# Loading vectors as rows, halving a wait, and reordering the opening of a one-core transformer-block kernel

## What is computed

```python
mod = (silu(c) @ wmod).reshape(4, 6, 1, 512)
sa, ca, ga, sb, cb, gb = (mod[:, i] for i in range(6))
ga, gb = sign-keeping max(|.|, 0.25) of each
h = layernorm(x) * (1 + ca) + sa
x = x + ga * attn_ref(h)      # ln1, shift-mix, r/k/v, out; then ln2, shift-mix, r2/k2/v2
h = layernorm(x) * (1 + cb) + sb
x = x + gb * ffn_ref(h)       # shared expert + top 2 of 8 experts
```

## Time and profile before

| | us |
|---|---|
| median of 3 runs (lowest, highest) | 1719.45 (1712.07, 1720.55) |
| the profiled execution's own time | 1702.0 |
| its span | 1700.3 |
| busy in it: TensorE, VectorE, ScalarE, GpSimd | 1643.6, 1326.2, 770.3, 417.9 |
| mean granted clock of TensorE | 0.993 |

### The profile page before, as it was taken

One profiled execution on the slowest core, in us unless ns is written; L12 is line 12 of the kernel. 1 busy time (PEld: TensorE's weight loads), 2 busy tenths in 40 slices (PEclk: granted clock), 3 DMA queues, 4 the chain that ended last, 5 costly groups with the idle time before them and its releaser, 6 DMA issues.

```text
span 1700.3 us, 26873 instructions
## 1 busy us (share of the span) xinstructions
PE 1643.6 (97%) x8817; PEld 1426.7 (84%) x8817; DVE 1326.2 (78%) x2553; ACT 770.3 (45%) x1138; POOL 417.9 (25%) x505
## 2 busy tenths in 40 slices
PE   4899999999989999999999999999999999999998
PEld 1578788888768888888888888999999999998997
DVE  3999999998698788888788775777777777776872
ACT  2444434333445555454545423555555555552331
POOL 2254444343322111323232351000000000006740
PEclk9999999999999999999999999999999999999999
DMA  9622222322544443655554689788878888866861
GB/s 317 222 76 93 80 99 74 99 74 75 202 149 154 151 149 123 223 183 201 180 197 173 223 318 312 240 287 298 286 259 279 284 299 285 266 219 215 277 209 38
DMA packets 138980, 335.32 MB, mean 197 GB/s; under 512 B 20568, under 2 KB 20568, under 8 KB 133232
## 3 DMA queue, kind: packets, MB, share of 16 engines
q1 hardware_dynamic: 103904, 248.09, 43.6%
q10 hardware_dynamic: 24720, 52.21, 8.6%
q0 software_dynamic: 10240, 33.56, 5.7%
HBM read 230.21 MB, written 103.60 MB: 196 GB/s over the span
## 4 chain that ended last, share of the span: by engine, by line
PE 73%; DVE 15%; DMA 4%; issue 3%; SPq 2%; ACT 2%; POOL 1%; DVEq 0%; ACTq 0%; POOLq 0%
PE bank L701 17%; PE bank L703 17%; PE bank L702 17%; PE bank L712 5%; PE bank L2412 5%; PE bank L2410 5%; PE bank L2411 5%; PE bank L2405 2%; DVE stage L1714 2%; DVE mix L1793 1%; DVE xm_lo L1799 1%; DMA expert_in_rows<-y_rows 1%; SPq L798 1%; DMA mod_rows<-ca_rows 1%; PE bank L2394 1%
## 5 line engine op out<-in xcount | busy, mean ns | idle before, releaser
L701 PE MATMUL bank<-gu_hi,ex_x_hl 128*128 128x352 f32 x1080 | 359.9, 333 | 0.1
L703 PE MATMUL bank<-gu_hi,ex_x_hl 128*128 128x352 f32 x1080 | 348.5, 323 | 0.0
L702 PE MATMUL bank<-gu_lo,ex_x_hl 128*128 128x352 f32 x1080 | 348.4, 323 | 0.0
L1281 POOL DMA_INDIRECT raw<-expert_out_rows,out_slots x64 | 74.9, 1170 | 536.7 <-DMA expert_out_rows<-y_rows 513.0
L701 PEld LDWEIGHTS bank<-gu_hi,ex_x_hl 128*128 128x128 f32 x1080 | 203.7, 189 | 0.4 <-issue 0.3
L702 PEld LDWEIGHTS bank<-gu_lo,ex_x_hl 128*128 128x128 f32 x1080 | 204.0, 189 | 0.0
L703 PEld LDWEIGHTS bank<-gu_hi,ex_x_hl 128*128 128x128 f32 x1080 | 203.3, 188 | 0.0
L1888 DVE TENSOR_TENSOR hid<-bank,sg_t 128x352 f32<-128x352 f32 x135 | 70.2, 520 | 126.8 <-PE bank L703 107.7
L2410 PE MATMUL bank<-dn_hi,hid_hi 128*128 128x512 f32 x405 | 161.7, 399 | 3.9 <-DVE hid_lo L1892 3.9
L2412 PE MATMUL bank<-dn_hi,hid_lo 128*128 128x512 f32 x405 | 160.0, 395 | 0.0
L2411 PE MATMUL bank<-dn_lo,hid_hi 128*128 128x512 f32 x405 | 158.7, 392 | 0.0
(11 more groups left out here) (257 smaller groups left out, 3835.9 us busy)
## 6 DMA issues: line engine op xcount, KB each, us to landing
raw<-in_ex_gu SPq DMA_DIRECT2D x40, 1408.0 KB, 6.5
raw<-in_ex_dn SPq DMA_DIRECT2D x40, 512.0 KB, 4.7
ex_x<-expert_in_rows SPq DMA_DIRECT2D x71, 256.0 KB, 6.3
expert_out_rows<-y_rows ACTq DMA_DIRECT2D x71, 256.0 KB, 6.1
h_rows<-h_t SPq DMA_DIRECT2D x64, 256.0 KB, 2.6
h_turned<-h_hl ACTq DMA_DIRECT2D x32, 512.0 KB, 3.0
ex_x_hl<-h_turned ACTq DMA_DIRECT2D x32, 512.0 KB, 3.7
x_t<-in_x SPq DMA_DIRECT2D x32, 256.0 KB, 2.7
```

The source lines that it names most:

```text
L701: pe.matmul(acc, act_hi[i], w_hi[i], start=(i == 0), stop=False)
L702: pe.matmul(acc, act_hi[i], w_lo[i], start=False, stop=False)
L703: last = pe.matmul(acc, act_lo[i], w_hi[i], start=False, stop=(i == chunks - 1))
L1281: pool.indirect_dma_start(rows[:, pair % 2, a, :], None, ys_d, bass.IndirectOffsetOnAxis(ap=out_slots[:, k, n:n + 1], axis=0)).then_inc(ar ...
```

## The change

1. The nine small vectors are loaded as 36 rows of 128 contiguous elements (4 rows each), all before anything else on ScalarE; TensorE turns the 36 rows with one transpose, and ScalarE copies the result to `vecs`.
2. The first third of `wmod` has two semaphores; the products of `sa` and `ca` start on the first two chunks when these are there.
3. SyncE's queue: tile 1 of x right after the first third of `wmod`; tiles 2 and 3 of x when tiles 0 and 1 were scaled, ahead of the other two thirds of `wmod`, with `v` between them and `o`, `u` among them; the rows of batches 1 to 3 in step 0; stores of the next two modulation rows in step 1 and the weights of channel mixing in step 2.
4. VectorE: for t < 0, `mixes` of tile t + 1 goes ahead of `scaled` of tile t + 3, and `x_stats` comes last; `r` and `k` are split in step -2, `v` in -1.
5. ScalarE and TensorE: `r`, `k` split after the modulation rows; the products of `ga`, `sb` in step -2, of `cb` in step 0 and of `gb` in step 1.

```diff
+        vec_rows = ga_rows[0:9 * C, 0:P]
...
+        wmod_first_in = sem("wmod_first_in")
...
-        MOD_BANK = {SA: psum[0], CA: psum[1], GA: psum[3], SB: psum[4], CB: psum[5], GB: psum[7]}
-        MOD_TURN = {SA: 1, CA: 2, GA: 5, SB: 6, CB: 7, GB: 8}
-        SPREAD_TURN = {SA: 3, CA: 4}
-        MOD_COPIED = {SA: 1, CA: 2, SB: 5, CB: 6}
+        MOD_BANK = {SA: psum[0], CA: psum[1], GA: psum[3], SB: psum[4], CB: psum[7], GB: psum[7]}
+        VECS_TURNED, VECS_COPIED = 1, 1
+        MOD_TURN = {SA: 2, CA: 3, GA: 6, SB: 7, CB: 8, GB: 9}
+        SPREAD_TURN = {SA: 4, CA: 5}
+        MOD_COPIED = {SA: 2, CA: 3, SB: 6, CB: 7}
...
-        SPLIT_IN_STEP = {-4: ["r", "k"], -2: ["v"], 0: ["o"], 5: ["r2"], 8: ["k2"], 11: ["v2"]}
+        SPLIT_IN_STEP = {-2: ["r", "k"], -1: ["v"], 0: ["o"], 5: ["r2"], 8: ["k2"], 11: ["v2"]}
...
                 for c in range(C):
...
-                                 io["wmod"][c * P:(c + 1) * P, 2 * q * D:2 * (q + 1) * D]).then_inc(wmod_in[q], 16)
+                                 io["wmod"][c * P:(c + 1) * P, 2 * q * D:2 * (q + 1) * D]
+                                 ).then_inc(wmod_first_in if q == 0 and c < C // 2 else wmod_in[q], 16)
             def load_weight(w):
...
+            sp.dma_start(x_t[:, 1, :], x_d[P:2 * P, :]).then_inc(x_in[1], 16)
...
-            sp.dma_start(x_t[:, 1, :], x_d[P:2 * P, :]).then_inc(x_in[1], 16)
-            load_wmod(1)
-            load_weight("v")
-            load_wmod(2)
-            load_weight("o")
-            sp.dma_start(u_bc[:], io["u"].partition_broadcast(P)).then_inc(u_in, 16)
             for m in (SA, CA):
...
-            sp.wait_ge(mod_out, 32)
-            for b in range(1, B):
-                sp.dma_start(flat(mod1[:, b]), mod_d[b, 0:2 * D].partition_broadcast(P)).then_inc(mod1_in, 16)
+            load_weight("v")
+            sp.wait_ge(*lnh_vec.done(1, "scaled"))
+            sp.dma_start(x_t[:, 1, :], x_d[3 * P:4 * P, :]).then_inc(x_in[1], 16)
+            load_wmod(1)
+            sp.dma_start(u_bc[:], io["u"].partition_broadcast(P)).then_inc(u_in, 16)
+            load_weight("o")
+            load_wmod(2)
             def later_mod(t):
                 if t.only(0):
+                    sp.wait_ge(mod_out, 32)
+                    for b in range(1, B):
+                        sp.dma_start(flat(mod1[:, b]), mod_d[b, 0:2 * D].partition_broadcast(P)).then_inc(mod1_in, 16)
+                if t.only(1):
...
+                if t.only(2):
...
                     for w in W2:
...
-                if t.only(2):
...
             def load_x(t):
-                if t.pair is None and t.n < 3:
+                if t.pair is None and t.n < 4:
...
                 if t.back(2).real():
...
             def load_vector(i):
-                act.dma_start(vecs[:, i, :], io[names[i]].rearrange("(c p) -> p c", p=P),
-                              allow_slow_non_contiguous=True).then_inc(vec_in, 16)
+                act.dma_start(vec_rows[i * C:(i + 1) * C, :], io[names[i]].rearrange("(c p) -> c p", p=P)).then_inc(vec_in, 16)
             def split_hi(w):
...
-            for i in (G1, B1, MUR, MUK, MUV):
+            for i in range(len(names)):
...
-            split_hi("r")
-            mod_row(SA)
-            split_hi("k")
-            mod_row(CA)
+            act.wait_ge(mod_mm, VECS_TURNED)
+            act.activation(vecs[:].rearrange("p i c -> p (i c)"), psum[7][:, 0:9 * C], ACT.Copy).then_inc(mod_act, 1)
+            for m in (SA, CA):
+                mod_row(m)
             for m in (SA, CA):
...
-            act.wait_ge(vec_in, 80)
-            for i in (G2, B2, MUR2, MUK2):
-                load_vector(i)
-            act.dma_start(wrt[:], io["wrT"].rearrange("(c p) e -> p c e", p=P)).then_inc(vec_in, 16)
+            act.wait_ge(mod_act, VECS_COPIED)
+            split_hi("r")
+            split_hi("k")
             def opening(t):
...
                 if t.only(-1):
...
+                    split_hi("o")
+                if t.only(0):
...
-                    split_hi("o")
+                if t.only(3):
+                    act.dma_start(wrt[:], io["wrT"].rearrange("(c p) e -> p c e", p=P)).then_inc(vec_in, 16)
                 for step, weights in SPLIT_IN_STEP.items():
                     if step > 0 and t.only(step - 1):
                         for w in weights:
...
-                (first_col, -1), (hhat, -2), (scaled, -3), (h_of, -3), (h_stats, -3), (h_moments, -3),
-                (x_stats, -4), (x_moments, -4), (mixes, -1), (mix_lo, -1))
+                (first_col, -1), (hhat, -2), (mixes, -1), (scaled, -3), (h_of, -3), (h_stats, -3), (h_moments, -3),
+                (mix_lo, -1), (x_stats, -4), (x_moments, -4))
             def time_step(t):
                 if t.pair is None and t.offset < 0:
...
-            for m in (SA, CA):
-                mod_product(m)
+            pe.wait_ge(vec_in, 16 * 9)
+            pe.transpose(psum[7][:, 0:9 * C], vec_rows, ident[0:9 * C, 0:9 * C]).then_inc(mod_mm, 1)
+            for half, arrived in enumerate((wmod_first_in, wmod_in[0])):
+                pe.wait_ge(arrived, 16 * (C // 2))
+                for m in (SA, CA):
+                    for c in range(half * C // 2, (half + 1) * C // 2):
+                        last = pe.matmul(MOD_BANK[m][0:B, :], cT[:, c, :], wmod[:, c, m * D:(m + 1) * D], start=(c == 0),
+                                         stop=(c == C - 1))
+                    if half:
+                        last.then_inc(mod_mm, 1)
             for m in (SA, CA):
...
-            mod_product(GA)
             def opening(t):
                 if t.only(-2):
+                    mod_product(GA)
...
-                if t.only(-1):
+                if t.only(0):
+                    pe.wait_ge(mod_act, SPREAD_TURN[CA])
...
-                    pe.wait_ge(mod_act, SPREAD_TURN[CA])
+                if t.only(1):
+                    pe.wait_ge(mod_act, MOD_COPIED[CB])
...
             def t1(t):
...
                 if t.only(0):
...
-                    pe.wait_ge(mod_act, MOD_COPIED[CB])
...
             def trw(t):
                 if t.back(1).real():
...
+                if t.only(0):
+                    pe.wait_ge(mod_act, MOD_COPIED[SB])
...
```

## The result

In ten runs each, the changed kernel has a median of 1723.01 us (1718.65 to 1726.99) against 1716.93 us before (1712.07 to 1720.55). The ratio is 1.0039, 95% interval [1.0025, 1.0053], so 6.7 us slower with an interval of 4.3 to 9.1 us. The profiled execution took a span of 1721.2 us.

The account below looks back on a forecast made before the run. VectorE was taken to set the pace from 50 to 100 us, before a fixed rhythm with TensorE full. Terms 0 + 1.1 + 5.1 = 6.2 us more, added to the median 1719.45, gave 1725.7; range 1713 to 1733.

Parts of the forecast that it names:

- -2 to +4: Bounds on the summed loss of 6.2 us at VectorE's later work; the case with them had chance 0.55.
- Vectors as rows: Opening loads on ScalarE: issues 0.55 us apart, 2.4 us per load, landing at 9.6, products from 10.0 instead of 10.28.
- S': VectorE's new start of scaling tile 0, claimed equal to S, the old start at 21.80 us.
- rival (b): Opening: vectors late, each load waiting a turn of 8 pieces of 4 KB; products 7 us later, 1732.7; chance 0.17.
- The halves bring nothing: First products on TensorE: `wmod`'s first half arrives before the vectors, so 16 passes still take 8.94 us; no gain.
- The store of `h`: SyncE's queue: tile 0's store lands at S' + 25 behind other loads; VectorE waits 6 us before `h_of` of tile 2.
- (a): Rival: the store of `h` isn't late, landing by S' + 19; 1719, or 1714 without the `hin` wait; chance 0.20.
- (c): Rival: both waits half as long because SyncE's traffic is faster; +1 to +3, within the main case, no separate chance.
- With the step's own 9.5 us ... unchanged: VectorE's step up to the split of `o` keeps its length, so that split comes 1.1 us later than before.
- The wait for `hin`: Step 2: `hin` lands at 95.2 behind channel-mixing weights; VectorE waits 5.1 us before `x2_of` of tile 0.
- Nothing takes that up: After the 5.1 us wait for `hin`, TensorE's whole rhythm shifts, so the wait passes on in full.
- TensorE's added products at nothing: Products of `cb`, `gb` in steps 0 and 1 fill TensorE's holes: cost nothing, up to 1 us if VectorE ran ahead.

Follow-up runs that it names:

- g: The changed kernel with the transpose of the 36 rows between the two halves of the first products: ratio 1.0034 to the kernel before, 5.8 us slower.
- Run a: The changed kernel with the last third of `wmod` issued after the stores of `h` of tiles 0 and 1: ratio 1.0020 to the kernel before, 3.4 us slower.
- c: The changed kernel with the last third of `wmod` behind the stores of `h` and the channel-mixing weights behind `hin`: ratio 0.9990 to the kernel before.
- b: The changed kernel with the three weights of channel mixing issued after `hin` of tile 0: ratio 1.0020 to the kernel before, 3.4 us slower.
- d: The kernel before, with only the channel-mixing weights moved from step 0 to step 2, ahead of `hin` of tile 0: ratio 1.0046, 7.8 us slower.
- e: The kernel before, with only the nine vectors loaded as rows and turned by the transpose: ratio 0.9986, 2.4 us faster.
- run h: The changed kernel with both weight loads moved back, the transpose between the halves, and the second third of `wmod` right after `k`: 1709.45 us against 1716.41, ratio 0.9964.
- the second timed difference: The changed kernel, with nothing altered, timed and profiled once more against the kernel before: ratio 1.0064, 10.9 us slower.

## Why the prediction was right

The direction, the mechanism (two waits on the order of SyncE's queue) and the size hold: 6.2 us forecast, 6.7 measured, and 8.7 in the trace at the point at which I summed, inside the -2 to +4 that I gave the sum. The forecast median, 1725.7, lies 2.7 us over the measured one, mostly because the kernel before came out at 1716.93 and not at 1719.45. By its steps:

- **Vectors as rows.** I had their landing at 9.6; the transpose is at 10.95, the last load was issued at 6.26. So a load takes not 2.4 us but up to 4.7, nearer to the lower bound, and the issues follow each other not at 0.55 but at 0.42 us on average. S' = S + 0.5 instead of S, which is within the spread of the traces. Nine turns of 32 KB one after the other would, by my estimate, have put the last landing at 17.3; it came 6 us before that, so the loads didn't wait for nine such turns in a row, and rival (b) is out. The Trainium skill says that an engine drains a whole packet of some 9 to 17 descriptors of one ring before it turns to the next (DMA: Bandwidth & Descriptors, Queues, rings and completion order). I had said that this gives the same figure as my 8 pieces of 4 KB, which holds only if a packet is that long and each load waits for a turn of its own. This trace doesn't bear out the two together, and doesn't tell which of them fails.
- **The halves bring nothing** was right (TensorE's 16 passes run through in 8.55 us), and g shows why: they would bring something if the vectors didn't stand ahead of them.
- **The store of `h`.** Forecast S' + 25 and a wait of 6 us; measured 48.26 = S' + 25.96 and 6.17. In 30.5 to 48.2 us DMA moved 361 GB/s, where I had reckoned with 378. Run a takes the wait away by taking bytes away. Rivals (a) and (c) are out: the store is late, and neither wait is half as long.
- **"With the step's own 9.5 us ... unchanged"** is the step that was off. From the first column of tile 1 (54.98) to the split of `o` it is 10.28 us: `hhat` of tile 2 waits 0.52 us for GpSimd at 56.91, since the statistics of tile 3, which GpSimd handles ahead of it, now come just before. (That `hhat` takes 1.19 us where it took 0.53 is mostly no loss: `scaled` ahead of it takes 0.73 where it took 1.22.) These 0.8 us, 0.5 for S' and 0.8 for the store make the split of `o` 3.2 us late, not 1.1. The same 0.52 us are in c, the version without the two waits.
- **The wait for `hin`.** Forecast 5.1 (3.5 to 6), measured 5.68; b takes it away and d makes it in the old kernel. "Nothing takes that up": the shift at tile 1 is still 8.7, with 8.75 at tile 0, and 8.8 at 500 us.
- **TensorE's added products at nothing**: c shows them free (40.8 us from the split of `o` to `x2_of` of tile 1, as before).
- **What I didn't see**: fewer small pieces let the large loads run faster (e). What it gives in the changed kernel no run shows by itself; ahead of the first store nothing of it is to be seen, since DMA moved less there than the 378 GB/s of my byte count.

The sum in the trace is 8.7 us (3.2 and 5.6) where I had 6.2 (1.1 and 5.1). That the first timed difference, 6.7, is so near to 6.2 is luck in part: both terms were forecast too small, and the second timed difference, 10.9, lies 4.7 us over the forecast.

## What to carry to other kernels

A store or load that an engine waits for can be as late as the bytes that its queue has ahead of it: here 5632 KB ahead of a store made a wait of 6.2 us and 3072 KB ahead of a load another of 5.7, though both transfers were 256 KB. So when loads are moved "out of the way" to a later point, look for the first small transfer behind that point, and put it ahead. And where a queue runs dry while it waits for a result, a load that needs no result can go into the gap; run h did that, but its gain is nearly all that of version c and of the edit of g, so no run here shows that this pays by itself.

## What was not expected of the hardware

Nine loads of 512 pieces of 4 bytes, 18 KB in all, slowed the large loads beside them (338 GB/s instead of 388 in 10.2 to 17 us, when the first five were under way), enough to move the end by 2.4 us (ratio 0.9986 [0.9973, 0.9999] without them). And the same program has a hole of about 10 us in TensorE's work near 1030 us on some occasions and not on others (9.42 against 19.31 us busy of 20), which moves the level of every kernel of a set by more than the change does. Only ratios within a set can be read.
